# Graph layers: three fixed edge blocks a window in place of two, and one small record a couple for TensorE's addresses

## The chip, the core and the metric

The kernel runs on one core of a Trainium2 chip. The metric is the device time of one execution in microseconds (us), as the median of several runs. Engines are written as the profile writes them: PE is TensorE (PEld its weight loads), DVE is VectorE, ACT is ScalarE, POOL is GpSimd, SP is SyncE; a name with q (PEq) is an engine's instruction queue, which also works out registers, waits and branches.

## The reference

There are 6250 nodes with 256 features and 100,000 edges, sorted by destination, each with one of 8 edge types. The destination of an edge is drawn as 6250 times the square of a uniform number, so low node numbers get far more edges than high ones.

```python
def _rgcn_conv(x, W, Wroot, b, src, dst, etype):
    xs = x[src]
    seg = dst * R + etype
    sums = segment_sum(xs, seg, N * R)
    cnt = segment_sum(ones, seg, N * R)
    mean = (sums / maximum(cnt, 1)[:, None]).reshape(N, R, -1)
    return x @ Wroot + b + einsum('nrd,rde->ne', mean, W)

x = x + conv2(relu(conv1(layernorm(x))))          # the two graph layers
x = x + ffn(layernorm(x))                         # 8 experts, top 2 of them per row
```

## The kernel before

**Tiles and windows.** The nodes lie in 49 tiles of 128 rows. A tile has 8 windows of 16 nodes, and 16 nodes times 8 types are the 128 segments that one window sums. Two windows are a couple, so a tile has 4 couples and a layer 196. The sorted edges are cut into 784 blocks of 128 edges. A window's span is the run of blocks that hold an edge of it: it begins at block `lo`, and two neighbours can share a block. Tiles are worked in the order of `RUNS`, which puts the long-span tiles between short-span ones:

```python
RUNS = ((0, 1), (13, 28), (1, 3), (28, 36), (3, 6), (36, 43), (6, 9), (43, 49), (9, 13))
```

A block that two runs share is gathered once for each, so a layer gathers 792 blocks.

**Gather.** POOL issues one indirect DMA for each block (L509). It brings the source rows of 128 edges, in a high and a low fp16 half, into one of 16 ring slots. SP hands out permissions in strict order (L394 to L399): for slot n it waits until PE has done the steps that read the old block (`freed`, L399), and then it waits for the landing of the block 8 further on and publishes it in `rows_ready` (`landed`, L395). The step count at which each block is free stands in `free_meta`, made in the setup from `last_row`, `left_row` and `turn_row`.

**Sums.** For a block and a window, DVE writes a 128 x 128 matrix of zeros and ones that tells which edge belongs to which segment, and PE multiplies it with the gathered rows in two matmuls, of 257 and 256 columns (`add_rows`, L1384 and L1385). The first two blocks of every window are fixed: DVE makes both matrices in one SCALAR_TENSOR_TENSOR (`first_blocks`, L1036), two couples ahead. Where a window has more than two blocks, both engines run a loop whose trip count is known only at run time: `more_blocks` on DVE (L1040 to L1044, one TENSOR_SCALAR a block, a couple ahead) and `more_sums` on PE (L1390 to L1396). They meet at `more_ready`.

**The rest of a couple.** Between the fixed blocks PE does the products of the means with the layer's weights, `product` (L1408, three 256-column matmuls each, 18 products a tile shared out by `SHARES` and `SPREAD`), and at the end of couple c the eight transposes of couple c-1, `turn` (L1400). The first product at the end of a couple raises `sums_done`. Then DVE takes the counts (L1066, L1069, layer 0 only), makes the fixed matrices of couple c+2, runs the loops of couple c+1 and writes the low halves of the means (L1079), for which `turn(c)` waits a couple later. ACT writes the high halves (L683) and copies the transposes out (L654). In couples 1 and 2 of a tile PE also transposes the tile's own rows (L1426).

**Records.** At the start of each couple PE loads eight registers (`load_couple`, L1376): four ring addresses, the two counts of rows to wait for, and the two ends of the loops. From them each matmul's address is worked out just ahead of it. DVE loads its own records once a tile, 20 registers (`load_meta`, L1027).

After the two layers come the routing and the expert part, which the diff doesn't touch.

## Time and profile before

| | us |
|---|---|
| median of 3 runs | 2932.6 (2931.3 to 2934.18) |
| span of the profiled execution | 3487.9 |
| first gather to last gather issued, both layers | 84.3 to 2637.8 |
| routing and experts after the layers | from about 2660 to 3487.9 |

The profiled execution's own time is the span of the profile: all that it shows lies between its first and its last instruction, and no other figure was taken of that execution. It is 555 us longer than the median of the runs, so shares and durations below belong to the profiled execution.

### The profile page before, as it was taken

The numbers are of one execution on the slowest core, as the hardware profiler recorded it, in microseconds if no ns is written. First come the engines' busy times: TensorE is split into PE (matmuls) and PEld (weight loads), VectorE is DVE, ScalarE is ACT, GpSimd is POOL, SyncE is SP. The second block draws the span as 40 slices with busy tenths as digits, with TensorE's granted clock in tenths as the row PEclk, the third lists the DMA queues.
The fourth block names the chain that finished last, engine by engine and source line by source line (L and its number), as shares of the span: only waits on it lengthen the run. The fifth ranks groups of instructions, "written<-read, shape, count | busy, mean of one in ns | idle before, by whom it ended". The sixth has DMA issues, their size and how long they took to land.

```text
span 3487.9 us, 82172 instructions
## 1 busy us (share of the span) xinstructions
PE 2472.0 (71%) x19212; PEld 1832.7 (53%) x19213; DVE 1780.8 (51%) x4984; ACT 1225.2 (35%) x2344; POOL 1862.5 (53%) x1980
## 2 busy tenths in 40 slices
PE   1346787678687786346776587687877428999999
PEld 0113565356365564114564365465656327888887
DVE  7324455345355454124454354354545338787777
ACT  5202343134243342012343143152432126555554
POOL 1666566655655554666556656655563543333333
PEclk9557999589799898557998798798997559999999
DMA  6223323233332232223333333333335234322222
GB/s 216 80 83 112 88 87 91 85 87 89 87 88 87 86 89 64 86 84 97 98 104 97 94 100 99 94 105 95 101 100 163 102 115 132 96 73 71 71 70 59
DMA packets 165489, 333.24 MB, mean 96 GB/s; under 512 B 36078, under 2 KB 102346, under 8 KB 165288
## 3 DMA queue, kind: packets, MB, share of 16 engines
q0 software_dynamic: 91632, 247.48, 24.1%
q1 hardware_dynamic: 39912, 41.03, 4.0%
q10 hardware_dynamic: 33872, 43.92, 3.9%
q8 instruction: 26, 0.43, 0.0%
q14 instruction: 47, 0.39, 0.0%
HBM read 285.39 MB, written 49.07 MB: 96 GB/s over the span
## 4 chain that ended last, share of the span: by engine, by line
PE 44%; issue 22%; DVE 10%; another core or an unknown queue 9%; DVEq 7%; SPq 2%; ACT 2%; DMA 1%; ACTq 0%; POOLq 0%; POOL 0%
PE more_banks L1408 13%; PE sum_banks L1384 9%; PE sum_banks L1385 7%; PE more_banks L1535 4%; PE sum_banks L1535 3%; PE more_banks L1400 3%; PE sum_banks L1545 3%; DVEq L1044 3%; DVEq L1041 2%; DVE sels L1044 2%; DVEq L1027 1%; DVE stage L1079 1%; DVE sels L1036 1%; PE sum_banks L1426 1%
## 5 line engine op out<-in xcount | busy, mean ns | idle before, releaser
L509 POOL DMA_INDIRECT ring<-table,tabs x1584 | 1526.9, 964 | 1046.4 <-SPq L399 670.0
L1384 PE MATMUL sum_banks<-ring,sels 128*128 x2348 | 726.6, 311 | 630.1 <-issue 420.1
L1408 PE MATMUL more_banks<-weights,stage 128*128 128x256 f16 x5292 | 919.1, 290 | 22.0 <-issue 21.4
L1385 PE MATMUL sum_banks<-ring,sels 128*128 x2348 | 732.2, 313 | 41.5 <-issue 38.7
L1384 PEld LDWEIGHTS sum_banks<-ring,sels 128*128 128x128 f16 (+1 forms) x2348 | 242.4, 103 | 928.2 <-issue 896.9
L683 ACT ACTIVATE stage<-sum_banks,inv 128x256 f16<-128x256 f32 x784 | 328.1, 473 | 789.5 <-issue 384.9
L1408 PEld LDWEIGHTS more_banks<-weights,stage 128*128 128x128 f16 x5292 | 531.1, 104 | 135.3 <-issue 37.1
L1036 DVE SCALAR_TENSOR_TENSOR sels<-lane,win_off,tabs 128x256 f16<-128x256 f16 x792 | 349.4, 482 | 422.1 <-remote 181.9
L654 ACT ACTIVATE stage<-more_banks 128x1024 f16<-128x1024 f16 x392 | 402.0, 1026 | 419.1 <-remote 405.6
L1044 DVE TENSOR_SCALAR sels<-lane,win_off,tabs 128x128 f16 x780 | 260.6, 334 | 495.8 <-issue 339.6
L1079 DVE SCALAR_TENSOR_TENSOR stage<-sum_banks,inv,stage 128x256 f16<-128x256 f32 x784 | 347.0, 479 | 57.2 <-issue 40.2
L1385 PEld LDWEIGHTS sum_banks<-ring,sels 128*128 128x128 f16 (+1 forms) x2348 | 241.9, 103 | 116.5 <-issue 68.0
L1400 PE MATMUL more_banks<-ident,stage 128*128 128x128 f16 x3136 | 272.3, 233 | 33.5 <-issue 21.9
L552 POOL DMA_INDIRECT out<-edge_work,lot_ids x106 | 109.2, 1030 | 332.3 <-DVE edge_work L1305 316.2
L681 ACT ACTIVATE stage<-sum_banks 128x256 f16<-128x256 f32 x196 | 75.2, 384 | 546.3 <-issue 231.2
L1400 PEld LDWEIGHTS more_banks<-ident,stage 128*128 128x128 f16 x3136 | 226.3, 105 | 69.9 <-issue 38.2
L1066 DVE TENSOR_SCALAR inv<-sum_banks 128x2 f32 (+1 forms) x196 | 31.1, 159 | 389.3 <-remote 150.1
L1545 PE MATMUL sum_banks<-weights,edge_work 128*128 128x256 f16 x1824 | 208.2, 275 | 8.9 <-DVE edge_work L1289 8.9
L760 ACT ACTIVATE stage<-sum_banks,edge_work,undo 128x256 f32<-128x256 f32 x212 | 117.2, 562 | 239.9 <-PE sum_banks L1535 211.2
L1545 PEld LDWEIGHTS sum_banks<-weights,edge_work 128*128 128x128 f16 x1824 | 179.4, 99 | 31.5 <-issue 9.8
L545 POOL DMA_INDIRECT edge_work<-out,old_ids x106 | 111.4, 1051 | 86.8 <-issue 77.6
L1287 DVE TENSOR_SCALAR edge_work<-stage,scales 128x256 f16<-128x256 f32 x212 | 75.5, 356 | 109.4 <-issue 59.9
(319 smaller groups left out, 2407.5 us busy)
## 6 DMA issues: line engine op xcount, KB each, us to landing
ring<-table,tabs POOLq DMA_INDIRECT x1584
weights<-L_ffn_W ACTq DMA_DIRECT2D x96, 178.5 KB
stage<-L_ffn_W ACTq DMA_DIRECT2D x16, 1024.0 KB, 5.0
edge_work<-lot_in SPq DMA_DIRECT2D x54, 260.0 KB
table<-edge_work ACTq DMA_DIRECT2D x49, 128.0 KB
lot_in<-sels SPq DMA_DIRECT2D x8, 260.0 KB
weights<-L_gnn_W SPq DMA_DIRECT2D x2, 1024.0 KB, 8.3
weights<-L_gnn_W ACTq DMA_DIRECT2D x2, 1024.0 KB
```

The source lines that it names most:

```text
L509: pool.indirect_dma_start(ring_rows[:, b % RING, 0:2 * D], None, tables[layer], bass.IndirectOffsetOnAxis(row_tab[:, b:b + 1], 0)).then_in ...
L654: act.activation(means[:, par, :, :, 2 * k * WIN:(2 * k + 2) * WIN].rearrange("p q r (v n) -> p v (q r) n", v=2), ps_turn[slot].rearrange( ...
L683: act.activation(mean16[:, slot, h, 0:D], ps_sum[slot][h][:, 0:D], ACT.Copy, scale=inv[:, ds(c * 2 + h, 1)]).then_inc(mean_high[layer], 1)
L1036: return v.scalar_tensor_tensor(sel[:, slot, h], lane16[:].unsqueeze(1).to_broadcast([P, 2, P]), win_off[:, ds(w, 1)], key_tab[:, ds((need ...
L1044: v.tensor_scalar(flat(sel_more[:, ds(block & (RING - 1), 1), :]), lane16[:], win_off[:, ds(w, 1)], key_tab[:, ds(block, 1)], ALU.add, ALU ...
L1079: v.scalar_tensor_tensor(mean16[:, slot, h, D:2 * D], ps_sum[slot][h][:, 0:D], inv[:, ds(c * 2 + h, 1)], mean16[:, slot, h, 0:D], ALU.mult ...
L1384: pe.matmul(to[:, 0:D + 1], hot, ring_row[:, ds(at + D, D + 1)], start=first, stop=last, skip_group_check=True)
L1385: return pe.matmul(to[:, 0:D], hot, ring_row[:, ds(at, D)], start=False, stop=last, skip_group_check=True)
L1400: out = [pe.transpose(ps_turn[slot][:, (4 * h + q) * P:(4 * h + q + 1) * P], mean16[:, slot, h, q * P:(q + 1) * P], ident16[:]) for h in r ...
L1408: return [pe.matmul(ps_out[par], rows[:, xp * KD + k, :], w16[:, wp, k, r * D:(r + 1) * D], start=part == PART_ORDER[0] and n == 0, stop=p ...
L1535: ins = pe.matmul(hid_bank[c % 4], up_sb[slot][:, wp, k, c * P:(c + 1) * P], lotT[:, zp, k, :], start=k == 0 and (wp, zp) == PART_PAIRS[0] ...
L1545: ins = pe.matmul(bank[2 + h][:, 0:D], hidT[:, hp, c, h * P:(h + 1) * P], down_sb[slot][:, wp, c, :], start=c == 0 and (hp, wp) == PART_PA ...
```

## The change

Each window now has three fixed blocks. The matrices of DVE are made three at a time (`first_blocks` over 128 x 384), PE does three `add_rows` for each window without a condition, and the loops run only for blocks four and on. PE waits for `lo + 3` rows instead of `lo + 2`, whether or not the window has a third block. The tables that say when a slot is free follow. Two records (`pe_row` with 8 words a couple, `meta` with 2 a window) become one, `bounds`, with 4 words a couple: `lo` and end of both windows. PE loads the four of the next couple ahead of `turn` in the couple before, and works out ring places and addresses from `lo`, the three blocks of a window together, ahead of the window's matmuls. To carry the record over a backward branch, the loop over tiles is written out in the layer with four kept registers. In couples with four products one of them moves from behind the fixed blocks of the first window to behind its loop.

```diff
+    FIXED = 3
+    RING_AT = 178304
...
-    SPREAD = {4: (1, 1, 0, 1, 1), 5: (1, 1, 1, 1, 1)}
+    SPREAD = {4: (1, 0, 1, 1, 1), 5: (1, 1, 1, 1, 1)}
...
-                sp.sem_inc(rows_ready[layer], 1)
+                sp.sem_inc(rows_ready[layer], FIXED - 1)
...
-            def first_blocks(layer, need, w, slot, h):
-                return v.scalar_tensor_tensor(sel[:, slot, h], lane16[:].unsqueeze(1).to_broadcast([P, 2, P]), win_off[:, ds(w, 1)],
-                                              key_tab[:, ds((need - 2).with_bounds(min_val=0, max_val=GATHERS - 1), 2)].unsqueeze(2).to_broadcast([P, 2, P]), ALU.add, ALU.is_equal)
-
-            def more_blocks(layer, need, end, w):
-                with v.If(end > need):
-                    with v.Fori(need & MASK, end) as i:
+            def first_blocks(lo, w, slot, h):
+                return v.scalar_tensor_tensor(sel[:, slot, h], lane16[:].unsqueeze(1).to_broadcast([P, FIXED, P]), win_off[:, ds(w, 1)],
+                                              key_tab[:, ds(lo, FIXED)].unsqueeze(2).to_broadcast([P, FIXED, P]), ALU.add, ALU.is_equal)
+
+            def more_blocks(layer, lo, end, w):
+                with v.If(end > lo + FIXED):
+                    with v.Fori((lo + FIXED) & MASK, end) as i:
...
-            def load_couple(c):
+            def load_couple(c, held=None):
                 loads[0] += 1
-                regs = [pe.alloc_register(f"pe_couple{loads[0]}_{k}") for k in range(8)]
-                pe.load(regs, pe_row[0:1, ds(c * 8, 8)])
-                at = [[pe.snap(regs[2 * b + h], donate=True, min_val=0, max_val=(RING - 1) * PITCH) for b in range(2)] for h in range(2)]
-                return regs, at, [pe.snap(r, donate=True) for r in regs[4:6]], [pe.snap(r, donate=True) for r in regs[6:8]]
+                regs = held or [pe.alloc_register(f"pe_couple{loads[0]}_{k}") for k in range(4)]
+                pe.load(regs, bounds_row[0:1, ds(c * 4, 4)])
+                return regs
+
+            def places(lo):
+                at = [(lo + b) % RING * PITCH for b in range(FIXED)]
+                for a in at:
+                    pe.compute_val(a * 2 + RING_AT)
+                    pe.compute_val((a + D) * 2 + RING_AT)
+                return at
+
+            rows_due = [pe.alloc_register(f"pe_rows_due{h}") for h in range(2)]
+
+            def rows_needed(lo, h):
+                pe.reg_alu(rows_due[h], lo + FIXED, 0, ALU.max)
+                return lo + FIXED
...
-                    regs, at, need, end = load_couple(c)
+                    own = regs is not kept
+                    lo = [pe.snap(r, donate=own) for r in regs[0:2]]
+                    end = [pe.snap(r, donate=own) for r in regs[2:4]]
+                    at = places(lo[0])
+                    picked_at, low_at = pe.compute_val(c + 1), pe.compute_val(c * 2)
+                    need = [rows_needed(lo[h], h) for h in range(2)]
...
-                        pe.wait_ge(rows_ready[layer], need[h] & MASK)
+                        if h == 1:
+                            at = places(lo[1])
+                        pe.wait_ge(rows_ready[layer], rows_due[h])
                         if h == 0:
-                            pe.wait_ge(sel_ready[layer], c + 1)
-                        add_rows(to, sel[:, slot, h, 0, :], at[h][0], True, False).then_inc(steps_done[layer], 1)
+                            pe.wait_ge(sel_ready[layer], picked_at)
+                        add_rows(to, sel[:, slot, h, 0, :], at[0], True, False).then_inc(steps_done[layer], 1)
                         some(3 * h)
-                        add_rows(to, sel[:, slot, h, 1, :], at[h][1], False, True).then_inc(steps_done[layer], 1)
+                        add_rows(to, sel[:, slot, h, 1, :], at[1], False, False).then_inc(steps_done[layer], 1)
+                        add_rows(to, sel[:, slot, h, 2, :], at[2], False, True).then_inc(steps_done[layer], 1)
...
                     first = some(4)
                     if first:
                         first[0].then_inc(sums_done[layer], 1)
+                    following = load_couple(c + 1, held)
+                    if first:
                         if age > 0 or k > 0:
-                            turn(c - 1, 1 - slot)
+                            turn(c - 1, 1 - slot, low_at)
...
-                graph_tiles(pe, tile_work)
+                regs = tile_work(0, 0, 0, load_couple(0), None)
+                tile_work(1, 1, 1, regs, kept)
+                with pe.Fori(1, PAIRS) as i:
+                    regs = tile_work(i * 2, 0, 2, kept, None)
+                    tile_work(i * 2 + 1, 1, 2, regs, kept)
+                regs = tile_work(TILES - 1, 0, 2, kept, None)
```

## Rows read from the trace of the kernel before

**Rows 1.** The page: busy time, share of the span, instructions of each engine.

```profile
PE 2472.0 (71%) x19212; PEld 1832.7 (53%) x19213; DVE 1780.8 (51%) x4984; ACT 1225.2 (35%) x2344; POOL 1862.5 (53%) x1980
```

**Rows 2.** Waits, longest first: engine, line waited at, releaser; total us, times, longest.

```profile
PEld sum_banks L1384 <- issue: 896.9, 1031, 8.3
POOL ring L509 <- SPq L399: 670.0, 574, 6.2
...
PE sum_banks L1384 <- DVE sels L1044: 152.4, 152, 4.8
...
PE sum_banks L1384 <- SPq L395: 25.9, 28, 8.0
```

**Rows 3.** Windows of layer 0, one for each run: busy us (x instructions), clock, DMA.

```profile
84.00:289.00 205.00, 77.21 (x266) 28.04 (x266) 69.05 (x189) 29.90 (x44) 127.98 (x128) 0.51 0.32 93
289.00:590.00 301.00, 233.38 (x1941) 171.82 (x1941) 163.21 (x471) 121.25 (x222) 180.40 (x188) 0.94 0.30 88
590.00:720.00 130.00, 75.02 (x370) 40.74 (x368) 40.34 (x119) 17.32 (x31) 80.05 (x84) 0.61 0.30 87
720.00:850.00 130.00, 112.12 (x1009) 88.79 (x1010) 78.60 (x230) 63.13 (x119) 75.63 (x79) 0.97 0.30 87
850.00:977.00 127.00, 78.47 (x480) 48.12 (x478) 45.41 (x138) 25.73 (x46) 77.00 (x81) 0.76 0.30 86
977.00:1084.00 107.00, 92.05 (x869) 74.84 (x867) 67.04 (x197) 56.75 (x105) 62.80 (x66) 0.98 0.30 88
1084.00:1184.00 100.00, 66.68 (x443) 44.72 (x442) 39.81 (x118) 23.86 (x45) 59.40 (x63) 0.79 0.29 86
1184.00:1268.00 84.00, 76.20 (x734) 63.31 (x733) 55.27 (x163) 48.13 (x90) 48.03 (x50) 0.99 0.31 88
1268.00:1372.00 104.00, 77.01 (x567) 51.95 (x566) 49.03 (x146) 32.14 (x61) 53.94 (x57) 0.89 0.26 77
```

**Rows 4.** Groups of instructions from 289 to 590 us.

```profile
L1044 DVE TENSOR_SCALAR sels<-lane,win_off,tabs 128x128 f16 x67 | 22.3, 333 | 11.8 <-issue 10.4 <-SPq L395 1.3
L1066 DVE TENSOR_SCALAR inv<-sum_banks 128x2 f32 (+1 forms) x60 | 9.5, 159 | 109.1 <-remote 44.1 <-PE more_banks L1408 44.0 <-issue 14.9
```

**Rows 5.** Groups of instructions from 1184 to 1268 us.

```profile
L1066 DVE TENSOR_SCALAR inv<-sum_banks 128x2 f32 x24 | 3.8, 159 | 26.3 <-PE more_banks L1408 12.4 <-issue 11.8 <-remote 2.1
L1044 DVE TENSOR_SCALAR sels<-lane,win_off,tabs 128x128 f16 x2 | 0.7, 334 | 0.4 <-issue 0.2 <-SPq L395 0.2
```

**Rows 6.** Timeline of 1203.3 to 1206.9 us: start, duration, instruction, count, idle before.

```profile
1203.22 0.88 DVE L1036 SCALAR_TENSOR_TENSOR sels<-lane,win_off,tabs 128x256 f16<-128x256 f16 x2
...
1203.58 0.27 PE L1384 MATMUL sum_banks<-ring,sels 128*128 x1
...
1203.69 0.27 PE L1385 MATMUL sum_banks<-ring,sels 128*128 x1
1204.00 0.95 POOL L509 DMA_INDIRECT ring<-table,tabs  x1 [1.08 <-SPq L399]
...
1204.30 0.31 DVE L1044 TENSOR_SCALAR sels<-lane,win_off,tabs 128x128 f16 x1 [0.20 <-issue]
...
1204.99 0.28 PE L1384 MATMUL sum_banks<-ring,sels 128*128 x1 [1.02 <-DVE sels L1044]
...
1205.26 0.94 POOL L509 DMA_INDIRECT ring<-table,tabs  x1 [0.30 <-issue]
...
1205.36 0.50 PE L1408 MATMUL more_banks<-weights,stage 128*128 128x256 f16 x3
1205.58 0.54 PEld L1400 LDWEIGHTS more_banks<-ident,stage 128*128 128x128 f16 x8
...
1206.38 0.22 PEld L1426 LDWEIGHTS sum_banks<-ident,edge_work 128*128 x2 [0.26 <-issue]
```

**Rows 7.** Line L509: count, duration min/median/max in ns, first and last start.

```profile
L509 POOL DMA_INDIRECT ring<-table,tabs x1584: 941/949/5499, 84.3 to 2637.8; - x198
```

**Rows 8.** Line L1376, PE's load of a couple's record, columns as in rows 7.

```profile
L1376 PEldq TENSOR_LOAD <-pe_row x392: 3/592/882, 110.2 to 2650.6; - x196
```

**Rows 9.** Line L662, ACT's load of one register.

```profile
L662 ACTq TENSOR_LOAD <-extremes x49: 279/285/303, 341.6 to 1383.2; - x49
```

**Rows 10.** Line L1384, the address work ahead of its matmul.

```profile
L1384 PEldq FUSED_REGOPS  x3128: 1/46/1392, 112.0 to 2654.2; - x196
```

## What the change should do to the time

> **What bounds the kernel now.** I read the page first. PE is busy 71% of the span, DVE 51%, POOL 53% [rows 1], an average over stages with different limits. The waits come next. The longest all lie around the sums: PE's weight loads idle 897 us at L1384 for nothing that the profile shows, PE idles 152 us there for DVE's L1044 (the loop's matrices), POOL idles 670 us for slots that SP has not given out (L399), and PE waits for rows published at L395 only 26 us [rows 2]. So the ring is full: gathers wait for PE and not PE for gathers, in the profiled execution.
>
> The third view cuts layer 0 at the ends of the nine runs [rows 3]. How many blocks and loops a stretch has I worked out from the reference's destinations, with the kernel's rule for `lo` and end: per layer 197 windows have at most two blocks, 130 have three and 65 have more; blocks beyond two are 390, beyond three 195. The trace agrees where I looked: 67 runs of L1044 in 60 couples from 289 to 590 us [rows 4], 2 in 24 couples from 1184 to 1268 [rows 5]. Two equations follow, 60a + 67b = 301 and 24a + 2b = 84 [rows 3 to 5]: a couple without loops costs a = 3.38 us, and a loop of one block b = 1.47 us. Its matmuls take 0.22 us of that, since L1385 starts 0.11 us after L1384 [rows 6], where the granted clock is 0.99 of 2.4 GHz; in the stretches of long windows it is down to 0.61 [rows 3], and the same two take up to twice that. In the example the last fixed matmul starts at 1203.69, the loop's first at 1204.99 because DVE's matrix came late, and the next product at 1205.36: 1.67 us where 0.11 would do [rows 6].
>
> The second limit lies close. POOL can start a gather every 1.26 us (1204.00 to 1205.26, no slot wait between) [rows 6]. From 289 to 590 us the tiles need 187 blocks, which at 1.26 is 236 us of the 301.
>
> **Profiled execution against timed runs.** The profile's own time is its span, 3487.9 us; the runs' median is 2932.6, 16% less. The gathers run from 84 to 2638 us [rows 7], 2554 us, and 934 lie outside. If those did not shrink at all, the layers would have 1998 us in a timed run, 1.26 per gather: exactly POOL's profiled step. The expert part is mostly PE at work and can shrink little; I take 5% for the outside, so 2045 us for the layers, 1020 each. So the timed run stands nearer the gather limit than the profile, unless POOL's step shrinks too. I bound that step by 0.95 (its busy time alone) and 1.26 [rows 6, 7] and take the middle, 1.10. What can't shrink is PE's streaming: 8 fixed matmuls and 13.5 products at 0.11 plus eight transposes, 0.5 us [rows 6], are 2.9 us a couple; with the loops' 780 blocks at 0.22 that is 1300 us in all. The other 1250 us shrink to 745, a factor 0.6. So a loop costs 0.22 + 0.6 x 1.25 = 0.97 us timed (bounds 0.22 and 1.47), a plain couple 2.9 + 0.6 x 0.48 = 3.19.
>
> **The change, part by part,** per layer, timed.
>
> Third fixed block. 197 windows pay two matmuls for nothing: 197 x 0.22 = +43 us on PE. In 130 windows the loop goes and the matmuls stay: -130 x 0.75 = -98. In the other 65 one block moves out of the loop: at the same 0.75, -49 (bound below 0, if those loops wait for gathers anyway).
>
> DVE. The instruction of 128 x 256 takes 0.44 us, two in 0.88 [rows 6]. A third more columns cannot cost less than nothing nor more than another half, 0.22: up to +0.44 a couple, against 195 TENSOR_SCALARs of 0.33 us less [rows 4], with their branches. DVE is 51% busy [rows 1], and after `sums_done` it has the whole next couple until `turn` asks, which becomes longer too. At nothing; were the cover gone, 0.4 x 196 = 80 us.
>
> PE's load. Eight registers take 592 ns [rows 8] and one on ACT 285 [rows 9]; on the line between them four take 417. More matters that it is issued ahead of `turn`, behind three queued products and the matmuls before them, where today it stands between `turn` and the sums: PE's loads idle 0.26 us ahead of L1426 in the example [rows 6]. I take -0.1 us a couple, bounds 0 and -0.4. The Trainium skill, page "DMA: Bandwidth & Descriptors", section "Latency and other measured facts", gives about 600 ns as the floor of a `tensor_load`. By it four registers would cost as much as eight, and only the move would be worth anything; ACT's 285 ns in this trace is below that floor.
>
> Addresses together. Today one register instruction of 46 ns stands ahead of each sum matmul, hidden by the one that runs [rows 10]. Now six addresses, 6 x 46 = 0.28 us, come in a bunch at a window's start, with modulo and products besides. For the second window the product behind the first window's loop (0.33 us) lies over them, which the new `SPREAD` provides for; for the first, the transposes (0.5 us). At nothing; the bound above is the whole bunch for each window, +0.28 x 392 = 110 us a layer.
>
> The wait for `lo + 3` rows asks for a block that may not be needed. PE waits for rows 26 us in all today [rows 2]; it costs nothing while the ring runs ahead, and one gather step a window where it doesn't. The setup's table changes are a few short rows: nothing.
>
> Now the stretches. Three of them (720 to 850, 977 to 1084, 1184 to 1268, with 84 couples, 24 one-block loops and 144 windows of at most two blocks) are PE's: +32 for the blocks, -18 for the loops, -8 for the loads, +6 together. The five others but the opening (60, 8, 12, 12 and 16 couples, 479 blocks) take 762 us in the profile [rows 3] and, with 84 x 3.19 + 24 x 0.97 = 291 for the three and some 150 for the opening taken off 1020, about 579 timed, 1.21 a block. They lose 106 loops and 57 blocks inside loops: -122, and +12 for 53 short windows, -11 for loads: 458 by PE. But 479 gathers at 1.10 take 527, and no ring keeps POOL wholly busy, so with 10 more 537: -42. The opening waits for gathers: -3. A layer gives 6 - 42 - 3 = -39, two give -78: 2932.6 - 78 = 2855 us. Of -121 that PE could gain there, the gather limit takes back about 80.
>
> In the profiled execution the same sum is larger. The three stretches come to 311 us of 321, the five by the larger of PE and gathers at 1.26 to 605 of 762; at 60% of these 167 us a layer, the span should come to about 3290.
>
> **Rivals.** (a) POOL's step shrinks with the rest, near 1.0. Then the five stretches reach about 490: -89 + 3 a layer, 2932.6 - 172 = 2760. For it: POOL's 0.30 us between gathers is labelled issue [rows 6], work of its queue that a profile may lengthen. Against: 0.95 of the step is the instruction itself.
>
> (b) The timed run is gather-bound already, step 1.21 or more. Then the loops' time is free in the five stretches and only the three move: +6 a layer, or +14 if the early load gives nothing: 2945 to 2960. It decides from a step of 1.21 on, since 479 x 1.21 is what those stretches take. For it: 1998 us over 1584 gathers. Against: 670 us of waits for slots [rows 2].
>
> (c) Slower by the address bunch: where its 0.28 us lies open at each second window, 196 x 0.28 = 55 us a layer comes on top where PE is the limit, about half the couples, 28 a layer: 2855 + 56 + 30 for the gain it eats in the five stretches = 2941; open at both windows, 3000. It decides once the queue's work for a couple passes PE's 3.4 us.
>
> (d) PE is the limit everywhere and the loops cost what their matmuls cost. Then only work counts: 2 x 43 us more, 3018. The Trainium skill, page "Perfetto Trace Analysis", section "Identifying Performance Opportunities", says that improving a kernel is improving its most-contended engine. That is PE here, by busy time and by weight loads (53%) [rows 1], and the change gives it 788 matmuls more. Against: the fit of 1.47 us a loop.
>
> (e) The loops don't vanish: at 65 windows a layer they stay by the data, more would need other destinations. Hardly possible.
>
> **How the numbers follow.** Forecast (2795 to 2905) 0.55; (a) 0.19; (b) 0.12; (c) 0.11; (d) 0.02; (e) 0.01. About 0.2% is what a measurement of this kernel can tell from no change, 2927 to 2938. The range runs from 2755, just past (a), to 2955, which takes in most of (b) and the milder (c). Faster: the forecast and (a), and a little of (b) and (c), 0.77. Same: 0.05, between them. Slower: 0.18.
>
> **What would show it.** In the profile after: DVE's loop line x390 instead of x780, PE's sum lines x2742 in place of 2348, a third more columns in `first_blocks` at 0.45 to 0.65 us. The last stretch of short tiles near 87 us, the long run after the opening near 245 us with POOL's gathers 1.3 us apart and its waits for L399 cut from 670 to under 400 us. PE's waits for L395 should rise: the gathers have become what is late next. The forecast is wrong if POOL waits for slots as long as before (then PE's queue or DVE holds the couple), or if the timed run gains nothing where the profile gains 200 us (then (b)). A gap of 0.3 us ahead of each window's first matmul would be (c).

## The result and the profile after

| kernel | median us | ratio to before (95%) |
|---|---|---|
| before | 2933.4 (2931.3 to 2934.2, 4 runs) | |
| after | 2956.2 (2955.3 to 2961.9, 4 runs) | 1.0084 (1.0070 to 1.0098) |

The change makes the kernel 0.8% slower, 22.8 us, and the runs of the two kernels do not overlap. The forecast was 2855, faster, with a range up to 2955.

The first thing to see is the span. The profile of after spans 2953.5 us, as long as its timed runs. The profile of before spanned 3487.9, 19% more than its runs, so the two can't be laid side by side. I had the unchanged kernel profiled once more, and it spanned 2929.6. Line L399, the semaphore step of SP's queue, shows the difference. In the profile shown before, the columns being count and duration min/median/max in ns:

```profile
L399 SPq EVENT_SEMAPHORE  x1552: 3/17/722, 112.7 to 2637.5; - x194
```

and in the second profile of the same kernel:

```profile
L399 SPq EVENT_SEMAPHORE  x1552: 17/17/17, 112.6 to 2132.1; - x194
```

In the first, steps of a queue that take 17 ns each time took up to 722. The engines' own instructions did not stretch: the gather's median is 949 ns in [rows 7] and 946 in the second, and DVE's instruction for two matrices takes 482 ns in both. All comparisons below are with the second.

Page of after: busy times (before: [rows 1]); the chain of work that ended last, as shares of the span, by engine and by line; and the three groups that matter (count, busy us, mean ns, idle before):

```profile
PE 2312.5 (78%) x20000; PEld 1863.8 (63%) x20001; DVE 1745.7 (59%) x4588; ACT 1192.2 (40%) x2344; POOL 1903.9 (64%) x1980
...
POOL 39%; PE 32%; issue 15%; DMA 7%; DVE 5%; SPq 1%; POOLq 1%; ACT 1%; DVEq 0%; ACTq 0%
POOL ring L509 35%; PE sum_banks L1572 7%; PE more_banks L1413 7%; DMA ring<-table,tabs 5%; PE sum_banks L1562 4%; PE more_banks L1562 4%; PE sum_banks L1389 3%; POOL lot_in L533 3%; PE sum_banks L1390 3%; PE more_banks L1405 2%; DMA out<-edge_work,lot_ids 1%; PE more_banks L1546 1%; SPq L405 1%; DVE weights L1210 0%; DVE stage L803 0%
...
L509 POOL DMA_INDIRECT ring<-table,tabs x1584 | 1569.8, 991 | 528.7 <-issue 438.9
...
L1029 DVE SCALAR_TENSOR_TENSOR sels<-lane,win_off,tabs 128x384 f16<-128x384 f16 x792 | 455.2, 616 | 267.1 <-PE more_banks L1413 242.9
...
L1037 DVE TENSOR_SCALAR sels<-lane,win_off,tabs 128x128 f16 x390 | 132.8, 341 | 438.6 <-SPq L395 428.5
```

The same of the unchanged kernel, second profile:

```profile
L509 POOL DMA_INDIRECT ring<-table,tabs x1584 | 1531.8, 967 | 544.3 <-issue 417.0
...
L1036 DVE SCALAR_TENSOR_TENSOR sels<-lane,win_off,tabs 128x256 f16<-128x256 f16 x792 | 349.6, 482 | 174.3 <-PE more_banks L1408 153.5
...
L1044 DVE TENSOR_SCALAR sels<-lane,win_off,tabs 128x128 f16 x780 | 271.4, 348 | 461.3 <-SPq L395 411.6
```

The loops went as meant (390 in place of 780). The chain that ended last runs through the gathers, and they grew: the same 1584 instructions take 991 ns in the mean, not 967, which is 38 us. Their medians are equal (946 ns), so some have become longer and most not at all.

Waits of after (before: [rows 2]):

```profile
PEld sum_banks L1389 <- issue: 393.5, 411, 5.2
...
PEld sum_banks L1389 <- SPq L395: 203.6, 216, 9.5
...
PE sum_banks L1389 <- SPq L395: 152.2, 198, 9.2
...
POOL ring L509 <- SPq L399: 52.5, 141, 6.4
```

Waits of the unchanged kernel, second profile:

```profile
PEld sum_banks L1384 <- issue: 629.5, 1029, 8.2
...
POOL ring L509 <- SPq L399: 86.2, 213, 6.3
...
PE sum_banks L1384 <- SPq L395: 22.3, 37, 7.9
```

The 670 us of waits for slots of [rows 2] belong to that one execution. In an ordinary one they are 86 before and 52.5 after, and each of these waits contains the 0.305 us that lie ahead of every gather; without it, 21 us are left before and 10 after, over 1584 gathers. So POOL hardly ever stands for want of a slot. PE's weight loads wait 394 us "for issue" instead of 630; most of what they no longer wait for the loop, they wait for rows (L395).

Windows of layer 1, from its first gather to its last, for after and then for the unchanged kernel (columns as in [rows 3]; POOL is the fifth pair):

```profile
1138.00:2164.00 1026.00, 805.40 (x7019) 625.01 (x7020) 525.14 (x1162) 371.04 (x679) 784.74 (x792) 0.88 0.41 118
```

```profile
1137.00:2141.00 1004.00, 807.01 (x6623) 582.68 (x6623) 543.79 (x1355) 370.55 (x679) 763.07 (x792) 0.88 0.41 121
```

Both have 792 gathers and 241 us in which POOL is idle, 0.305 us ahead of each. The layer is 22 us longer, and POOL's busy time is 21.7 us longer. In the median a gather costs 0.946 + 0.305 = 1.25 us, and 792 of them 990: **the layer's length is the gather chain.** Over both layers the two profiles, 24 us apart, add up to within 1 us: gathers are 38 us longer, waits for slots 12 us shorter, the pause between the layers is 4 us shorter, and what follows the last gather is 1 us longer.

Windows of layer 0 of after, cut at the ends of the nine runs (before: [rows 3]), and the sum:

```profile
245.00:491.00 246.00, 210.47 (x2046) 177.33 (x2046) 155.14 (x404) 117.24 (x223) 188.43 (x190) 1.00 0.38 108
...
593.00:707.00 114.00, 110.54 (x1104) 96.99 (x1102) 80.76 (x217) 62.85 (x120) 87.21 (x89) 0.98 0.38 110
...
963.00:1048.00 85.00, 81.89 (x836) 72.68 (x835) 60.53 (x162) 47.14 (x90) 63.61 (x63) 1.00 0.38 107
...
sum 1039.00, PE 812.51 PEld 625.99 DVE 590.30 ACT 406.42 POOL 785.03; mean PE 90.28 PEld 69.55 DVE 65.59 ACT 45.16 POOL 87.23
```

Long run 246 us, last short stretch 85: the numbers that I had named, beside a wrong total. The unchanged kernel takes 251 and 82 for them and 1038 for the layer, so nothing came off. In layer 0 the longer gathers (+17 us) are partly hidden by the shorter waits for slots (-12).

### The profile page after: what moved, and what is told of

Same layout as the page of the kernel before. It is cut to its first block, busy times and chain, and to the rows that moved or that the text cites. A ratio compares the mean times of both kernels' runs of the same rounds, so it can differ in the third digit from the quotient of the medians.

```text
span 2953.5 us, 77529 instructions
## 1 busy us (share of the span) xinstructions
PE 2312.5 (78%) x20000; PEld 1863.8 (63%) x20001; DVE 1745.7 (59%) x4588; ACT 1192.2 (40%) x2344; POOL 1903.9 (64%) x1980
## 3 DMA queue, kind: packets, MB, share of 16 engines
q0 software_dynamic: 91632, 247.48, 28.6%
## 4 chain that ended last, share of the span: by engine, by line
POOL 39%; PE 32%; issue 15%; DMA 7%; DVE 5%; SPq 1%; POOLq 1%; ACT 1%; DVEq 0%; ACTq 0%
POOL ring L509 35%; PE sum_banks L1572 7%; PE more_banks L1413 7%; DMA ring<-table,tabs 5%; PE sum_banks L1562 4%; PE more_banks L1562 4%; PE sum_banks L1389 3%; POOL lot_in L533 3%; PE sum_banks L1390 3%; PE more_banks L1405 2%; DMA out<-edge_work,lot_ids 1%; PE more_banks L1546 1%; SPq L405 1%; DVE weights L1210 0%; DVE stage L803 0%
## 5 line engine op out<-in xcount | busy, mean ns | idle before, releaser
L509 POOL DMA_INDIRECT ring<-table,tabs x1584 | 1569.8, 991 | 528.7 <-issue 438.9
L1389 PE MATMUL sum_banks<-ring,sels 128*128 x2742 | 764.3, 294 | 413.9 <-DVE sels L1037 223.1
L1413 PE MATMUL more_banks<-weights,stage 128*128 128x256 f16 x5292 | 855.8, 278 | 0.0
L1390 PE MATMUL sum_banks<-ring,sels 128*128 x2742 | 767.1, 294 | 0.0
L1389 PEld LDWEIGHTS sum_banks<-ring,sels 128*128 128x128 f16 (+1 forms) x2742 | 275.4, 100 | 630.4 <-issue 393.5
L1029 DVE SCALAR_TENSOR_TENSOR sels<-lane,win_off,tabs 128x384 f16<-128x384 f16 x792 | 455.2, 616 | 267.1 <-PE more_banks L1413 242.9
L1413 PEld LDWEIGHTS more_banks<-weights,stage 128*128 128x128 f16 x5292 | 518.3, 99 | 83.6 <-issue 4.4
L1037 DVE TENSOR_SCALAR sels<-lane,win_off,tabs 128x128 f16 x390 | 132.8, 341 | 438.6 <-SPq L395 428.5
L1072 DVE SCALAR_TENSOR_TENSOR stage<-sum_banks,inv,stage 128x256 f16<-128x256 f32 x784 | 341.1, 476 | 4.0 <-issue 2.6
L1390 PEld LDWEIGHTS sum_banks<-ring,sels 128*128 128x128 f16 (+1 forms) x2742 | 276.9, 101 | 34.4
L1405 PE MATMUL more_banks<-ident,stage 128*128 128x128 f16 x3136 | 252.9, 227 | 2.3 <-issue 0.5
L1405 PEld LDWEIGHTS more_banks<-ident,stage 128*128 128x128 f16 x3136 | 214.8, 101 | 25.9 <-issue 9.0
L1562 PE MATMUL sum_banks<-edge_work,weights 128*128 128x256 f16 x912 | 113.6, 274 | 7.6 <-ACT stage L760 5.0
```

The costliest lines, as they stand in the source:

```text
L509: pool.indirect_dma_start(ring_rows[:, b % RING, 0:2 * D], None, tables[layer], bass.IndirectOffsetOnAxis(row_tab[:, b:b + 1], 0)).then_in ...
L1029: return v.scalar_tensor_tensor(sel[:, slot, h], lane16[:].unsqueeze(1).to_broadcast([P, FIXED, P]), win_off[:, ds(w, 1)], key_tab[:, ds(l ...
L1037: v.tensor_scalar(flat(sel_more[:, ds(block & (RING - 1), 1), :]), lane16[:], win_off[:, ds(w, 1)], key_tab[:, ds(block, 1)], ALU.add, ALU ...
L1072: v.scalar_tensor_tensor(mean16[:, slot, h, D:2 * D], ps_sum[slot][h][:, 0:D], inv[:, ds(c * 2 + h, 1)], mean16[:, slot, h, 0:D], ALU.mult ...
L1389: pe.matmul(to[:, 0:D + 1], hot, ring_row[:, ds(at + D, D + 1)], start=first, stop=last, skip_group_check=True)
L1390: return pe.matmul(to[:, 0:D], hot, ring_row[:, ds(at, D)], start=False, stop=last, skip_group_check=True)
```

## The experiments

Beside the medians I worked out numbers from each trace's rows of the gathers: the **mean** of L509; **long**, what the gathers of layer 0 and of layer 1 took over 945 ns each, summed; **slots**, what POOL was idle ahead of gathers over 306 ns each, likewise (without the first of a layer); **last**, when the last gather starts, in us from the span's start. Long and slots are us for layer 0 / layer 1. Last is there because some experiments leave data out of the sums, and with other sums, rows of the expert part go to other experts. The time after the last gather is 788 to 794 us in the kernels whose sums are complete, but 782 in dve2 and 801 in narrow3. The line that writes the expert part's rows back shows it, in after, dve2 and narrow3:

```profile
L552 POOL DMA_INDIRECT out<-edge_work,lot_ids x106 | 109.6, 1034 | 320.5 <-DVE edge_work L1298 304.3
...
L552 POOL DMA_INDIRECT out<-edge_work,lot_ids x104 | 107.9, 1038 | 315.4 <-DVE edge_work L1299 299.6
...
L552 POOL DMA_INDIRECT out<-edge_work,lot_ids x108 | 112.4, 1040 | 324.0 <-DVE edge_work L1298 307.5
```

All other kernels here have 106. For dve2 and narrow3, what an edit is worth in the layers is read from last, each from one execution.

| kernel | median us | ratio (95%) | mean ns | long | slots | last |
|---|---|---|---|---|---|---|
| before_again | 2931.7, one run | | 967 | 20 / 16 | 21 / 0 | 2140.5 |
| after | 2956.2 | 1.0070 to 1.0098 | 991 | 37 / 37 | 10 / 0 | 2163.1 |
| rec2 | 2918.3 | 0.9928 to 0.9961 | 965 | 16 / 17 | 8 / 0 | 2123.6 |
| narrow3 | 2954.4 | 1.0054 to 1.0088 | 985 | 30 / 34 | 6 / 0 | 2149.8 |
| split_wait | 2950.4 | 1.0042 to 1.0076 | 987 | 33 / 34 | 10 / 1 | 2156.2 |
| dve2 | 2917.4 | 0.9932 to 0.9965 | 967 | 22 / 15 | 15 / 4 | 2133.9 |
| dve3 | 2948.5 | 1.0034 to 1.0068 | 987 | 35 / 33 | 5 / 0 | 2155.6 |
| after_21 | 2937.3 | 1.0003 to 1.0022 | 972 | 26 / 19 | 18 / 3 | 2145.2 |
| after_ts1 | 2935.3 | 1.0001 to 1.0019 | 971 | 22 / 20 | 18 / 3 | 2142.1 |
| half_before | 2900.6 | 0.9869 to 0.9902 | 934 | | | 2108.3 |
| half_after | 2907.5 | 0.9895 to 0.9928 | 951 | | | 2115.7 |
| rec2_ts | 2936.9 | 0.9996 to 1.0015 | 956 | 12 / 6 | 38 / 0 | 2144.1 |
| rec2_late | 2923.5 | 0.9951 to 0.9980 | 967 | 19 / 17 | 11 / 0 | 2128.4 |
| rec2_mix | 2979.5 | 1.0139 to 1.0167 | 959 | 17 / 5 | 8 / 71 | 2184.6 |

Layer 1 shows the chain at its cleanest: no kernel of the first three lines waits there for a slot, and from the unchanged kernel to after its gathers' first-to-last time grew from 1003.7 to 1024.8 us, 21.1, where long grew 20.9.

**before_again and rec2: the records alone.** rec2 is after with two fixed blocks:

```diff
-    FIXED = 3
+    FIXED = 2
-    SPREAD = {4: (1, 0, 1, 1, 1), 5: (1, 1, 1, 1, 1)}
+    SPREAD = {4: (1, 1, 0, 1, 1), 5: (1, 1, 1, 1, 1)}
-                        add_rows(to, sel[:, slot, h, 1, :], at[1], False, False).then_inc(steps_done[layer], 1)
-                        add_rows(to, sel[:, slot, h, 2, :], at[2], False, True).then_inc(steps_done[layer], 1)
+                        add_rows(to, sel[:, slot, h, 1, :], at[1], False, True).then_inc(steps_done[layer], 1)
```

> The kernel before, unchanged, for a second profile. The profile of the changed kernel spans 2953.5 us, as long as its timed runs, while that of the kernel before spanned 3487.9 against 2933. If that excess belongs to the one profile, this one should span about 2931. Theory G (the gathers already bound the kernel before, at POOL's 1.25 us a gather): the five stretches of long and middle windows take 1.25 to 1.30 us a block, and POOL's waits for slots at L399 come to under 150 us. Rival P (PE and DVE held it by their loops): 1.30 or more, with over 300 us of waits at L399.

> The changed kernel with two fixed blocks again: only the small records, the load ahead of the transposes and the bunched addresses are left, with the old SPREAD. Theory G: the bunch costs nothing and PE gains about 0.1 us a couple where it is the limit, so 2915 to 2933. Rival A (the bunched address work is what made the change slower): 2950 or more.

The unchanged kernel ran as its median says. The records, the early load and the bunched addresses together are worth 15 us. Hence the third block costs 38 (2918.3 to 2956.2). In layer 0 POOL's waits for slots fell from 21 to 8 us, which is where most of the 15 us lie: they are the moments when PE is late in giving rows back. rec2 beats both kernels.

**narrow3 and split_wait: is the third block dear on PE?** In narrow3 the matmuls of the third block have 16 columns (so its rows count only for those). In split_wait PE waits for `lo + 2` rows first and for `lo + 3` only ahead of the third block.

```diff
+                def add_few(to, hot, at):
+                    pe.matmul(to[:, 0:16], hot, ring_row[:, ds(at + D, 16)], start=False, stop=True, skip_group_check=True)
+                    return pe.matmul(to[:, 0:16], hot, ring_row[:, ds(at, 16)], start=False, stop=True, skip_group_check=True)
```

```diff
-                        pe.wait_ge(rows_ready[layer], rows_due[h])
+                        pe.wait_ge(rows_ready[layer], rows_two[h])
...
+                        pe.wait_ge(rows_ready[layer], rows_due[h])
```

> The changed kernel, in which the third fixed block's two matmuls stream 16 columns in place of 257 and 256 (the sums leave most of that block's data out); all waits and counts stay. Theory G: what the change lost is streaming on PE in the short-window stretches, 168 windows a layer of 0.2 us, so 60 us less, about 2895. Rival W (the wait for the third block's rows is what costs): 2945 or more.

> The changed kernel, but each window waits for lo + 2 rows ahead of its first block and for lo + 3 only ahead of its third. Theory G: 2950 to 2960, as the changed kernel. Rival W: the loss of 23 us comes back, 2935 or less.

Neither is the main cost. For narrow3 I had expected 2895; its median is only 1.8 us below after's, but its expert part has more to do and takes 11 us longer. Its last gather starts 13 us earlier than after's, so some 13 us is what streaming is worth in the layers. The wait is worth 5.8 us in the median and 7 by the last gather; whether the two add was not tried. Even if they did, about half of the 38 us would be left.

**dve2 and dve3: DVE's instruction by itself.** dve2 is after in all of PE's work, but DVE makes only two matrices (128 x 256) a window, and the third is zero throughout, so third blocks are left out of the sums. dve3 is rec2 in all of PE's work, and its sums are complete, but DVE makes three matrices, of which PE uses two. The edit of dve3:

```diff
-                return v.scalar_tensor_tensor(sel[:, slot, h], lane16[:].unsqueeze(1).to_broadcast([P, FIXED, P]), win_off[:, ds(w, 1)],
-                                              key_tab[:, ds(lo, FIXED)].unsqueeze(2).to_broadcast([P, FIXED, P]), ALU.add, ALU.is_equal)
+                return v.scalar_tensor_tensor(sel[:, slot, h], lane16[:].unsqueeze(1).to_broadcast([P, 3, P]), win_off[:, ds(w, 1)],
+                                              key_tab[:, ds(lo, 3)].unsqueeze(2).to_broadcast([P, 3, P]), ALU.add, ALU.is_equal)
```

> The changed kernel, but DVE makes only the first two of the three matrices, in an instruction of 128 x 256; the third stays zero (third blocks drop out of the sums). PE, its waits and the gathers are those of the changed kernel. Theory L (a gather instruction on POOL is held up while DVE's matrix instruction runs, and the longer instruction holds it longer; the gathers are the chain that sets the layers' time): the mean gather falls from 991 to about 967 ns and the time from 2956 to about 2930. Rival S (the third block's steps and waits on PE): mean gather as it comes, time 2945 or more.

> The kernel with the new records and two fixed blocks, which ran at 2918 us with a mean gather of 965 ns, but DVE makes three matrices in one instruction of 128 x 384, of which PE uses two. Only DVE's instruction is longer. Theory L: mean gather 985 ns or more, time 2945 to 2955. Rival S: within 5 us of 2918, since DVE has slack.

This pair settles it. The wide instruction alone takes rec2 from 2918.3 to 2948.5, +30. Taking it away from after gives 39 back in the median (26 were expected), but some 9 of these come after the last gather, from dve2's smaller expert part; in the layers it is 29 (last, 2163.1 to 2133.9). The rest of the 38 is PE's third block: 8 us from dve3 to after (2948.5 to 2956.2), and 10 by the last gather from rec2 to dve2. The page's rows of dve3, first, and of rec2:

```profile
L509 POOL DMA_INDIRECT ring<-table,tabs x1584 | 1563.6, 987 | 527.4 <-issue 424.2
...
L1027 DVE SCALAR_TENSOR_TENSOR sels<-lane,win_off,tabs 128x384 f16<-128x384 f16 x792 | 455.2, 616 | 135.0 <-PE more_banks L1411 111.6
```

```profile
L509 POOL DMA_INDIRECT ring<-table,tabs x1584 | 1528.9, 965 | 530.5 <-issue 417.3
...
L1027 DVE SCALAR_TENSOR_TENSOR sels<-lane,win_off,tabs 128x256 f16<-128x256 f16 x792 | 349.7, 482 | 141.2 <-PE more_banks L1411 117.7
```

DVE is not late in either: it waits as much for PE ahead of its instruction. POOL's gather instruction becomes longer beside DVE's. Sorted by whether a matrix instruction of this kind overlaps them, gathers (but for the two over 3 us in each trace) take in the mean 983 and 951 ns in the unchanged kernel, 979 and 950 in rec2, 1025 and 952 in dve3, 1037 and 950 in after. Those that don't meet one are alike everywhere. Timeline of after in layer 1 (start, duration, instruction, count, idle before):

```profile
1499.20 0.95 POOL L509 DMA_INDIRECT ring<-table,tabs  x1 [0.30 <-issue]
1499.48 1.15 DVE L1029 SCALAR_TENSOR_TENSOR sels<-lane,win_off,tabs 128x384 f16<-128x384 f16 x2 [1.34 <-PE more_banks L1413]
1500.45 1.00 POOL L509 DMA_INDIRECT ring<-table,tabs  x1 [0.30 <-issue]
...
1501.76 0.95 POOL L509 DMA_INDIRECT ring<-table,tabs  x1 [0.30 <-issue]
1502.72 1.15 DVE L1029 SCALAR_TENSOR_TENSOR sels<-lane,win_off,tabs 128x384 f16<-128x384 f16 x2 [1.30 <-PE more_banks L1413]
1503.01 1.15 POOL L509 DMA_INDIRECT ring<-table,tabs  x1 [0.30 <-issue]
...
1504.46 0.95 POOL L509 DMA_INDIRECT ring<-table,tabs  x1 [0.30 <-issue]
```

The pair of 1499.48 costs the gather of 1499.20 nothing and the next one 0.05 us; the pair of 1502.72 costs the gather of 1503.01 0.20 us. The gathers after it have slipped by as much, since nothing ahead of them was idle. What decides is which of the two started first. When the gather of 1503.01 started, an instruction of 0.616 us had been running since 1502.72 and had 0.33 us left.

The trace's rows of L509 and L1029 show this as a rule. In after, 280 gathers start at least 0.1 us into one of these instructions while at least 0.13 us of it is left. Every one of them exceeds the median by what is left of the instruction less 0.127 us, within 15 ns, and by 0.39 us at most. Together that is 56 of the 64 us by which gathers exceed their median (again without the two over 3 us). Of the 287 gathers that such an instruction meets only after they have started, none exceeds it by more than 5 ns. The unchanged kernel has 154 gathers caught in this way, with 19.5 of 26.5 us; rec2 has 151, with 18 of 23.5. So a longer instruction costs twice over: it catches more gathers, and each of them has more of it left to wait for.

Not every DVE instruction does this. Those for the low halves of the means (L1072 in after) are SCALAR_TENSOR_TENSORs of 476 ns too, but read one of their two tensors from PSUM, where the sums lie, while both tensors of the matrix instructions lie in SBUF. In after 201 gathers start inside one of them in the same manner, and none exceeds the median by more than 11 ns:

```profile
717.57 0.88 DVE L1072 SCALAR_TENSOR_TENSOR stage<-sum_banks,inv,stage 128x256 f16<-128x256 f32 x2
717.85 0.95 POOL L509 DMA_INDIRECT ring<-table,tabs  x1 [0.30 <-issue]
```

**after_21 and after_ts1: length or inputs?** Both make the three matrices in two instructions, 128 x 256 and 128 x 128. In after_21 the second is a SCALAR_TENSOR_TENSOR like the first, in after_ts1 a TENSOR_SCALAR, whose keys come as a scalar and not as a second tensor.

```diff
+                v.scalar_tensor_tensor(sel[:, slot, h, 0:2, :], lane16[:].unsqueeze(1).to_broadcast([P, 2, P]), win_off[:, ds(w, 1)],
+                                       key_tab[:, ds(lo, 2)].unsqueeze(2).to_broadcast([P, 2, P]), ALU.add, ALU.is_equal)
+                return v.tensor_scalar(sel[:, slot, h, 2, :], lane16[:], win_off[:, ds(w, 1)], key_tab[:, ds(lo + 2, 1)], ALU.add, ALU.is_equal)
```

> The changed kernel, but the three matrices of a window come from an instruction of 128 x 256 and one of 128 x 128, both with two tensor inputs. If the length of one instruction is what holds a gather up, the mean gather falls from 991 to 975 ns or less and the time to 2925 to 2940. If it is the time in which DVE runs instructions with two tensor inputs, in a row or not, the mean gather stays at 985 ns or more and the time at 2950 or more.

> The same, but the third matrix comes from a TENSOR_SCALAR of 128 x 128, which has one tensor input. Length alone: as after_21. Inputs: the mean gather falls to 965 to 972 ns, as with two-block instructions, and the time to 2915 to 2930, less what DVE's longer work costs.

Length: cut in two, the same matrices hold the gathers up far less (972 and 971 ns, against 991), although DVE is busy longer. It is as the rule has it: after_21's two-input instructions still catch 251 gathers, but with 24 us in all instead of 56. The kind of the short instruction makes 2 us of difference, with overlapping intervals; after_ts1's mean of 971 ns lies in the range that I had given to either reading, and its time, 2935, lies above the 2930 that inputs allowed before DVE's longer work is counted. Both give back 19 to 21 us of the 38. The rest lies in gathers still a little longer than rec2's (long 42 to 44 us in both layers, against 33) and in waits for slots (21 us against 8), presumably since DVE's longer work makes PE late.

**skip_before and skip_after: what the loops were worth.** From the second turn of the ring on, the gathers into slots 5, 7, ... 15 are left out in both (290 of 792 a layer; those slots keep their first rows), and everything else stays.

```diff
+    SKIPPED = range(5, RING, 2)
...
+                    if b >= RING and b % RING in SKIPPED:
+                        continue
```

> The kernel before, with the gathers into ring slots 5, 7, 9, 11, 13 and 15 left out after the first turn of the ring (291 of 792 a layer; their blocks are summed from old rows). POOL then needs some 630 us a layer, so PE and DVE with their loops set the time. Theory L: the layers fall well below the 1010 to 1038 us of before, to 850 to 980. Rival: they stay above 1000, if gathers weren't the chain.

> The changed kernel with the same gathers left out. If a loop was worth 0.75 us more than its matmuls, as the prediction took it, 260 loops and 130 blocks fewer against 394 needless blocks of 0.22 us make this the faster of the two by 150 to 210 us. If loops cost near nothing beside their matmuls, it is slower than skip_before by up to 86 us.

2805.0 (ratio 0.9542 to 0.9574) and 2596.6 (0.8836 to 0.8866). With over a third of the gathers gone the same change is worth 208 us. Layer 0, from its first gather to PE's last sums, takes 997 and 887 us. What I expected of PE's side was there; the gathers covered it. It also shows the other side of the cover: taking 580 gathers of 1.25 us, 725 us, from before saves 128 only, as then PE and DVE with their loops are the limit.

**half_before and half_after: a cheaper gather?** Gathers of 64 rows in place of 128; the other 64 rows of a block are never brought.

```diff
-                    pool.indirect_dma_start(ring_rows[:, b % RING, 0:2 * D], None, tables[layer],
-                                            bass.IndirectOffsetOnAxis(row_tab[:, b:b + 1], 0)).then_inc(gathered[b % RING], 16)
+                    pool.indirect_dma_start(ring_rows[0:64, b % RING, 0:2 * D], None, tables[layer],
+                                            bass.IndirectOffsetOnAxis(row_tab[0:64, b:b + 1], 0)).then_inc(gathered[b % RING], 16)
```

> The kernel before with gathers of 64 rows in place of 128 (half of the edges' rows stay 1). If the gathers set the time (theory L), the layers get much shorter, until PE and DVE with their loops are the limit: first gather to last, 1004 to 1030 us a layer now, falls to 850 to 980. Rival: within 10 us of the kernel before, if anything but POOL's instruction paces the layers.

> The changed kernel with gathers of 64 rows. If removing 260 loops is worth what the prediction took it for (0.75 us each against 0.22 for every needless block), this one is the faster of the two by 60 to 120 us a layer once the gathers are out of the way. If the loops were never worth that, it is within 20 us of half_before or behind it.

half_before missed its 850 to 980 us a layer: the step shrinks by some 35 ns only, so these kernels don't relieve the chain as I meant, and half_after can't tell what the loops are worth. Half the rows, and a gather takes 912 ns (median) in place of 946: it is priced by the instruction. The change still loses, 7 us instead of 23.

**rec2_ts, rec2_late, rec2_mix: variants of the best.** rec2_ts makes each fixed matrix by its own TENSOR_SCALAR. rec2_late loads PE's record behind `turn`. rec2_mix is rec2 in layer 0 and rec2_ts in layer 1.

```diff
+                for b in range(FIXED):
+                    ins = v.tensor_scalar(sel[:, slot, h, b, :], lane16[:], win_off[:, ds(w, 1)], key_tab[:, ds(lo + b, 1)], ALU.add, ALU.is_equal)
+                return ins
```

```diff
-                    following = load_couple(c + 1, held)
-                    return following
+                    return load_couple(c + 1, held)
```

> The new records with two fixed blocks (2918 us), where DVE makes the two matrices with two TENSOR_SCALARs of 128 x 128 in place of one instruction of 128 x 256 with two tensor inputs. Theory L1 (it is the length of the single instruction that holds a gather up): mean gather below 960 ns and 5 to 15 us less than 2918. Rival L2 (any DVE instruction on these tables holds it as long as it runs in a row): within 5 us of 2918, or slower by DVE's extra 0.2 us a window.

> The new records with two fixed blocks, but PE loads the next couple's record behind the transposes and not ahead of them. If the 15 us that the records gain came from the early load, this returns to 2928 to 2934; if they came from fewer registers and fewer address instructions, it stays within 5 us of 2918.

> The new records with two fixed blocks (2918 us), layer 0 as there, and in layer 1 two TENSOR_SCALARs in place of the instruction with two tensor inputs. In rec2_ts the layer 1 was 10 us shorter than in rec2 and layer 0 was 30 us longer, because DVE was late there. So 2908, and 2918 if the two layers' gains don't add.

Layers are measured here from their first gather to PE's last sums. rec2_ts was to be 5 to 15 us faster than rec2 and is 19 slower. It has the shortest gathers of the full-sized runs (956 ns) and a layer 1 of 998.4 us, 10 less than rec2's, but a layer 0 of 1051.0, 30 more, with 38 us of waits for slots: there DVE, with two instructions more a couple, is what I take to be late. rec2_late shows the early load to be worth about 5 of the 15 us, with overlapping intervals. rec2_mix was to join the better halves and missed: its layer 1 takes 1075.2 us. The gathers there are short (long 5), but POOL waits for slots, 183 us over both layers with the 0.305 us ahead of each gather, 79 without:

```profile
POOL ring L509 <- issue: 377.6, 1233, 2.3
...
DVE sels L1041 <- SPq L395: 327.4, 429, 4.7
...
POOL ring L509 <- SPq L399: 183.3, 349, 5.1
...
DVE sels L1033 <- issue: 101.0, 37, 4.6
```

Its DVE instructions in layer 1 are those of rec2_ts, which took 998.4. But ahead of the fixed matrices (L1033) DVE stands 101 us for nothing that the profile shows, up to 4.6 us at a time, where rec2_ts has 4.7 us of this in all. That makes DVE late and accounts for the slots; what holds it there stays open.

## Why the prediction was wrong

**"So the timed run stands nearer the gather limit than the profile, unless POOL's step shrinks too. I bound that step by 0.95 (its busy time alone) and 1.26 [rows 6, 7] and take the middle, 1.10."** This is the step that failed first. The step does not shrink: 946 to 949 + 305 ns in the median of every trace with whole gathers. The sum in the prediction had already met it, 1998 us over 1584 gathers, 1.26 each, and called it the profiled step. The right reading was that a stretched profile stretches what the stretching acts on. Queue steps of 17 ns took up to 722; instructions of engines did not. So the factor of 0.6 could apply to PE's and DVE's queues, and POOL's part stood. With 1.25 the five stretches are gather-bound from the start: rival (b). For the same reason rival (a), a step near 1.0, fell.

**"Three of them ... are PE's: ... +6 together."** Wrong too, and by rule and not by size. A maximum of PE and gathers for each stretch takes POOL as idle in the short ones. It isn't: there the ring of 16 refills what the long stretches drained, and POOL gathers through all nine. The sum over a layer is one chain of 792 gathers. In layer 0 the three stretches took 301 us before and 298 after, the five 577 and 581, for forecasts of 291 and 579 before and 297 and 537 after. So rival (b)'s 2945 to 2960 holds the time by luck, and its mechanism only in part. That the loops' time is free it had right. But it had +6 to +14 a layer from PE, and dve2, which has all of PE's new work, ends its gathers 7 us before the unchanged kernel: the third block's 8 to 10 us are more than paid by the records.

**DVE's wider instruction, "at nothing".** Right as far as DVE's own time goes: +0.13 us (616 ns against 482), inside the 0 to 0.22, and hidden. Wrong in what it does to another engine. It costs 30 us (dve3; 29 in the layers by dve2). With 15 gained by the records and 8 lost by the third block, that makes the 23 us of the result. I had no such term. The window of [rows 6] has a case of it in the kernel before, a gather of 1.07 us that starts 0.25 us into a matrix instruction:

```profile
1206.26 0.88 DVE L1036 SCALAR_TENSOR_TENSOR sels<-lane,win_off,tabs 128x256 f16<-128x256 f16 x2
...
1206.51 1.07 POOL L509 DMA_INDIRECT ring<-table,tabs  x1 [0.30 <-issue]
```

**Loops and third blocks.** For PE the terms were about right. With the load they came to -115 a layer, -230; with gathers thinned out the change brought -208, and the third block's streaming, forecast at 86 us of PE's time, cost some 13 us in the layers while covered (narrow3). The loops simply did not lie on the chain.

**The load.** 332 ns in place of 592, and the early place worth about 5 us in all (rec2_late, intervals overlapping). The forecast was 0.1 us a couple, 39 us, but under the gather chain only layer 0's slot waits could yield it. The prediction gave the Trainium skill, page "DMA: Bandwidth & Descriptors", section "Latency and other measured facts", with a floor of about 600 ns for a `tensor_load`; the trace does not agree, with 332 ns for four registers:

```profile
L1369 PEldq TENSOR_LOAD <-bounds x392: 327/332/424, 110.8 to 2163.2; - x196
```

**Addresses (rival c).** Fell: rec2 has the bunch of four and is 15 us faster than before; dve2 has the bunch of six, and its gathers end 7 us earlier. **PE everywhere (rival d).** Fell with skip_after, where the loops are worth far more than their matmuls. **Loops that stay (rival e).** Fell with the count of 390. **The wait for three rows.** It was rightly named as dear only where the ring does not run ahead, but the ring does not run ahead: PE's waits at L395 rose from 22 to 152 us. Most of that would have been waited for elsewhere; splitting the wait gains 5.8.

On what would show it: loops x390, `first_blocks` at 616 ns, 245 and 85 us in the two stretches, gathers 1.25 us apart and L399 under 400 all came true. The first two say only that the edit was made, and the others told nothing, since in an ordinary execution they nearly held before the change (251 and 82 us, 1.25, 86). Of the signs of a wrong forecast one came: the profile became 534 us shorter and the timed runs gained nothing, which the prediction had put down to (b).

## What to carry to other kernels

When a profile is much longer than the runs, find out which instructions stretched, and leave the others at their full length: an engine whose own instructions did not stretch may be the limit of the timed run. With a ring between producer and consumer, sum the producer over the whole layer and don't take a maximum for each stretch. Where POOL's indirect DMAs are the chain, a longer DVE instruction with both tensors in SBUF costs even if DVE has time; try the same work in shorter ones, and look at the gather's mean beside its median. When an experiment leaves data out, look whether a later part of the kernel still does the same amount of work before comparing whole times.

## What the runs showed of the hardware

An indirect DMA costs POOL's engine and queue 1.25 us for 128 rows and 1.22 for 64, so it is paid by the instruction. The Trainium skill, page "Perfetto Trace Analysis", section "What "DMA-bound" means", lists the sequencer of the issuing engine as one of the things a kernel can be bound on, apart from the DMA engines. The trace agrees: POOL's DMA queue keeps the 16 DMA engines 28.6% busy, and in layer 1 POOL issues 792 gathers with only 0.305 us between them.

POOL's indirect DMA is held up by a DVE instruction with two tensors in SBUF that was already running when it started, by what is left of that instruction less 0.127 us: up to 0.26 us behind instructions of 482 ns (rec2) and 0.39 behind those of 616 (after). It is not held up by one that starts later (287 gathers, at most 5 ns), nor by one of 476 ns that reads one tensor from PSUM (201 gathers, at most 11 ns). The Trainium skill, page "SBUF — State Buffer", sections "SBUF: two separate sides" and "Who interferes with whom", says that GpSimd, which writes the descriptors of its own DMAs, shares a port pair with VectorE, and that whichever comes second is blocked until the other's instruction ends. It names two kinds of VectorE instruction that take the pair: those in a 2-port mode, and those with two inputs in SBUF, these only against GpSimd's reads. The trace agrees with the second kind: the gather reads its row numbers from SBUF (`tabs`), and of two SCALAR_TENSOR_TENSORs of about the same length only the one with both tensors in SBUF holds it. That the port is the cause is argued from the page and not shown.
